# Layer 0's scores of a pair in two PSUM banks, softmax up to four units ahead in the first chunk, and positions set anew

## The chip, the cores and the metric

The kernel runs on one core of one Trainium2 chip. The metric is the device time of one execution in microseconds (us). The program is one launch; its engines are TensorE (PE), VectorE (DVE), ScalarE (ACT), GpSimd (POOL) and SyncE (SP, which only issues DMAs). Each engine works through its own list of instructions in order and meets the others at semaphores.

## The reference

Four layers run one after the other on x (8 sequences of 256 tokens, 512 features). Cut to what matters:

```python
# layer 0: RMS norm with conditioning, 8 query heads of 64 and ONE key/value head, rope, then a gated MLP
q, k, v = h @ Wq.T, h @ Wk.T, h @ Wv.T
scores = rope(q) @ rope(k).T / 8          # 256 x 256 of each head and sequence
attn = softmax(scores, axis=-1)
x = x + (attn @ v) @ Wo.T
x = x + (silu(h2 @ Wg.T) * (h2 @ Wu.T)) @ Wd.T     # 2048 wide
# layer 1: layer norm, 16 heads of 32, normalised q and k, attention and a gelu MLP of 2048
# layer 2: layer norm, 16 query heads and 4 key heads of 32, sparse mask, attention, no MLP
# layer 3: 8 expert blocks, layer norm, silu, projection
```

Inputs and outputs are float32. A softmax needs the maximum of each row of scores, the exponentials, their sum, and a division.

## The kernel before

**Tiling.** The 2048 tokens are four batches of 512 (two sequences each), features lie on the partitions. Attention of layer L on batch n is an *item*; `ORDER` has 12 items, the first four are layer 0 on batches 0 to 3 (called chunks here). An item is 16 *units* g: four groups t of heads, two sequences b, two query tiles of 128 tokens (the last bit of g). Units g and g+1 with g even are a *pair*: same heads, same sequence. A large matmul is taken as three products of rounded halves, so a projection of 128x512 is 12 matmuls.

**Steps of a unit, by the name in the plan.** `scores` (for a pair: 12 matmuls in layer 0, two heads of 64) on PE; `softmax`: on DVE a `reduce_max` per head and a multiply by -0.125 into NM, then on ACT an exponential per head from PSUM to a buffer of SS, with its sum; `normalise`: reciprocal of the sum on DVE, a multiply of each head by it on POOL; `turn`: four transposes of a bank on PE, and a copy to PT by ACT (g even) or DVE (g odd) in layer 0; `values` (for a pair, one unit after its second turn): 8 matmuls, then copies to CX by ACT and DVE; after an item, `out` (48 matmuls). Projections of q and k: `ro1` (12 matmuls, copied out by ACT), `ro2` (rotation matmul, sine product and sum on DVE, cosine product on POOL), `qs` (rounded part on DVE, rest on POOL) or `ks`; in layer 1 `un1`, `un2`, `un3` stand in their place. `split` (POOL) prepares a weight piece that came by `load`, `store` and `fetch` (SP) keep and bring it back.

**Order.** Nothing schedules at run time. `Plan.at` gives every step a position, in units; the steps are sorted by it, and every engine walks the one list and emits its part of each step. `unit(g)` stands at position g and adds, in this order: scores of g+2 (if even), normalise g+1, values g-3 (if g is odd), turn g, softmax g+2 (`AHEAD = 2`). The table `PLACE` holds the positions of everything else. Chunk 0 has no MLP to run beside it; from chunk 1 on the MLP of the batch before stands between the units.

**Memory.** PSUM has 8 banks of 128x512 float32, given out by the pool `dp` first in, first out; the next user of a bank waits for the last reader of the one before. A pair of layer 0 takes four banks of which each holds one head of one unit in its first 256 columns; layers 1 and 2 also take four, with a head's two units side by side. SS has three buffers of probabilities, taken in turn (`ssr`), NM four sets of maxima and sums. HM is the MLP's input (rounded part and rest, 16 KB of a partition); it is first written by the last norm steps (`nfin`) of the MLP of batch 0, at position 19.7.

## Time and profile before

| | us |
|---|---|
| median of 3 runs (2042.67 to 2044.4) | 2044.22 |
| span of the profiled execution | 2053.7 |
| PE busy in it | 1912.4 (93%) |
| DVE / ACT / POOL busy | 1110.8 / 1027.7 / 795.9 |

The profiled execution's span is 9.5 us above the median of the timed runs, so a difference read in the trace is carried over to the median as a difference, not as a ratio. In the profile each engine has its busy time; a wait is idle time of an engine just before an instruction, named by what released it. Times in the trace are counted from the start of the span.

### The profile page before, as it was taken

The numbers are of one execution on the slowest core, as the hardware profiler recorded it, in microseconds if no ns is written. First come the engines' busy times: TensorE is split into PE (matmuls) and PEld (weight loads), VectorE is DVE, ScalarE is ACT, GpSimd is POOL, SyncE is SP. The second block draws the span as 40 slices with busy tenths as digits, with TensorE's granted clock in tenths as the row PEclk, the third lists the DMA queues.
The fourth block names the chain that finished last, engine by engine and source line by source line (L and its number), as shares of the span: only waits on it lengthen the run. The fifth ranks groups of instructions, "written<-read, shape, count | busy, mean of one in ns | idle before, by whom it ended". The sixth has DMA issues, their size and how long they took to land.

```text
span 2053.7 us, 35242 instructions
## 1 busy us (share of the span) xinstructions
PE 1912.4 (93%) x12880; PEld 1512.5 (74%) x12880; DVE 1110.8 (54%) x3184; ACT 1027.7 (50%) x2474; POOL 795.9 (39%) x1094
## 2 busy tenths in 40 slices
PE   5889999999999999999899989989999989988987
PEld 3567777788888878887778777768876768855565
DVE  5655535644553365345664676574554675366363
ACT  3542423433343344443565465555567565468665
POOL 4556662111124243234667554326332432243230
PEclk9899999999999999999999999989999999989989
DMA  7336677555444534444345433433433335322311
GB/s 249 110 129 209 229 249 264 181 196 190 172 160 177 181 134 171 156 158 153 135 174 187 158 118 139 171 114 107 165 113 134 127 110 195 130 81 69 124 63 52
DMA packets 98795, 314.84 MB, mean 153 GB/s; under 512 B 11584, under 2 KB 13376, under 8 KB 97088
## 3 DMA queue, kind: packets, MB, share of 16 engines
q1 hardware_dynamic: 98624, 312.58, 43.7%
q8 instruction: 104, 1.70, 0.3%
q14 instruction: 67, 0.55, 0.1%
HBM read 242.55 MB, written 66.58 MB: 151 GB/s over the span
## 4 chain that ended last, share of the span: by engine, by line
PE 76%; DVE 10%; POOL 4%; ACT 4%; issue 3%; DMA 1%; SPq 0%; POOLq 0%; DVEq 0%; ACTq 0%
PE B L194 69%; PE B L197 7%; DVE FB L215 2%; POOL R L212 1%; DVE SS L218 1%; DVE T L212 1%; POOL SS L209 1%; ACT SS L200 1%; DVE FB L212 1%; POOL FB L212 1%; DMA ST<-in_wpack 1%; DVE PT L206 1%; ACT FB L200 1%; DVE HA L215 1%; POOL W L212 1%
## 5 line engine op out<-in xcount | busy, mean ns | idle before, releaser
L209 POOL TENSOR_SCALAR SS<-SS,NM 128x256 f32<-128x256 f32 (+1 forms) x640 | 290.2, 471 | 747.3 <-DVE NM L224 747.1
L194 PE MATMUL B<-HM,W 128*128 128x512 f32 x2304 | 540.1, 395 | 9.2 <-DVE HM L215 5.7
L194 PEld LDWEIGHTS B<-HM,W 128*128 128x128 f32 x2304 | 436.5, 190 | 105.6 <-issue 5.0
L194 PE MATMUL B<-G,W 128*128 128x512 f32 x1536 | 391.6, 405 | 8.1 <-POOL W L212 4.3
L194 PEld LDWEIGHTS B<-G,W 128*128 128x128 f32 x1536 | 286.1, 191 | 76.1 <-issue 10.7
L200 ACT ACTIVATE SS<-SS,NM 128x256 f32<-128x256 f32 (+1 forms) x512 | 240.5, 471 | 121.2 <-DVE NM L218 120.8
L194 PE MATMUL B<-HA,W 128*128 128x512 f32 x864 | 229.6, 418 | 6.1 <-DVE HA L212 4.4
L197 PE MATMUL B<-ident,SS 128*128 128x128 f32 x1152 | 180.6, 294 | 41.1 <-POOL SS L209 33.6
L194 PEld LDWEIGHTS B<-HA,W 128*128 128x128 f32 x864 | 170.6, 202 | 45.9 <-issue 5.4
L212 DVE TENSOR_TENSOR G<-FB,G 128x512 fp32r<-128x512 f32 x128 | 99.5, 780 | 165.3 <-ACT G L200 165.2
L197 PEld LDWEIGHTS B<-ident,SS 128*128 128x128 f32 x1152 | 129.9, 147 | 77.6 <-issue 41.1
L212 POOL TENSOR_TENSOR R<-R,few 128x16 f32<-128x16 f32 (+2 forms) x57 | 119.3, 2095 | 141.5 <-DVE R L209 141.4
L200 ACT ACTIVATE PT<-B 128x512 f32<-128x512 f32 x160 | 95.0, 593 | 149.6 <-PE B L197 147.4
L212 POOL TENSOR_TENSOR W<-ST,W 128x512 fp32r<-128x512 f32 x119 | 159.8, 1343 | 9.9
L200 ACT ACTIVATE G<-FB 128x512 fp32r<-128x512 f32 x128 | 80.9, 632 | 162.3 <-DVE FB L212 160.3
L209 POOL TENSOR_SCALAR W<-ST 128x512 fp32r<-128x512 f32 x119 | 80.3, 675 | 201.4 <-PE B L194 125.2
L212 DVE TENSOR_TENSOR FB<-FB,B 128x512 f32<-128x512 f32 x64 | 44.0, 687 | 191.5 <-PE B L194 175.8
L200 ACT ACTIVATE FB<-B 128x512 f32<-128x512 f32 (+2 forms) x148 | 85.6, 592 | 105.3 <-PE B L194 104.8
L194 PE MATMUL B<-CX,W 128*128 128x512 f32 (+1 forms) x624 | 136.3, 376 | 0.3 <-issue 0.3
L212 DVE TENSOR_TENSOR X<-X,B 128x512 f32<-128x512 f32 (+1 forms) x100 | 66.4, 665 | 128.8 <-PE B L194 128.7
L200 ACT ACT_TABLE_LOAD x99 | 127.0, 1283 | 4.8 <-PE B L194 2.4
L194 PEld LDWEIGHTS B<-CX,W 128*128 128x128 f32 x624 | 111.3, 190 | 22.8 <-issue 1.9
(109 smaller groups left out, 2654.0 us busy)
## 6 DMA issues: line engine op xcount, KB each, us to landing
W<-kept SPq DMA_DIRECT2D x357, 512.0 KB, 4.2
kept<-W SPq DMA_DIRECT2D x119, 512.0 KB, 4.6
ST<-in_wpack SPq DMA_DIRECT2D x139, 256.0 KB, 2.9
Y<-in_adaw SPq DMA_DIRECT2D x12, 1024.0 KB, 6.8
FB<-FB SPq DMA_DIRECT2D x52, 64.0 KB, 2.6
X<-in_xT SPq DMA_DIRECT2D x1, 3072.0 KB, 13.0
out_xT<-X SPq DMA_DIRECT2D x12, 256.0 KB, 2.1
FB<-in_pos SPq DMA_DIRECT2D x4, 256.0 KB, 6.0
```

Source lines behind the costliest of these rows:

```text
L194: return self.real.matmul(*a, **k) if self.real is not None else self
L197: return self.real.transpose(*a, **k) if self.real is not None else self
L200: return self.real.activation(*a, **k) if self.real is not None else self
L206: return self.real.tensor_copy(*a, **k) if self.real is not None else self
L209: return self.real.tensor_scalar(*a, **k) if self.real is not None else self
L212: return self.real.tensor_tensor(*a, **k) if self.real is not None else self
L215: return self.real.scalar_tensor_tensor(*a, **k) if self.real is not None else self
L218: return self.real.tensor_tensor_reduce(*a, **k) if self.real is not None else self
```

## The change

1. **Two banks for a pair of layer 0.** The scores of a pair now lie as in the other layers: one bank for a head, the first unit in columns 0 to 255, the second in 256 to 511. With the even unit DVE reads both: two `reduce_max` of 2x256 and one multiply for both units; with the odd unit DVE does nothing. Both banks come free with the odd unit's exponentials.
2. **Softmax further ahead in chunk 0.** `ahead(g)` is 4 for units 0 to 9, 3.5, 3 and 2.5 for the pairs 10, 12 and 14, and 2 from unit 16 on (the last pair's value is 2 too, so nothing is deepened at the end). Scores and softmax get positions of their own, `normalise` of a deep unit moves one unit earlier, and the projections of q and k move with `ahead`.
3. **Buffers.** SE overlaps HM's memory and gives two more buffers of probabilities for units below 16. NM has six sets. The first writing of HM waits for the last transposes of unit 15. The waits of the later MLP inputs are named by the right key (before, the key named nothing and no wait was made); the matmul waited for lies 40 to 94 steps ahead of the first one that waits, in both plans.
4. **Positions.** About half of the numbers in `PLACE` change, most of them by less than 0.3 of a unit. Beside chunk 0 this swaps some neighbours; the 16 `un2` of q in layer 1 stand some steps earlier, and in the last item two `second` come before two `out`.

```diff
 AHEAD = 2
+DEEP = 4
+FIRST_DEEP, LAST_DEEP = 16, 192
 LAG = 2
...
 PLACE = {
...
-    "q1": [-1.273, 0.351, 1.427],
+    "q1": [-1.247, -0.466, 1.37],
-    "start": [-12.43, 6, -2.831, -0.049],
+    "start": [-12.43, 7.191, -2.895, 0.384],
...
+def deep(g):
+    return g < FIRST_DEEP or g >= LAST_DEEP
+def ahead(g):
+    return min(DEEP, max(AHEAD, AHEAD + (FIRST_DEEP - pair(g)) / 4, AHEAD + 0.5 + (pair(g) - LAST_DEEP) / 4))
+def banks_of(g):
+    return keys(g) * HEADS[layer(g)] // 512
 def keys(g):
...
-    def __init__(self, dp, f, nm, ss):
-        self.dp, self.f, self.nm, self.ss = dp, f, nm, ss
-        self.work, self.steps, self.raw_values = [], [], {}
+    def __init__(self, dp, f, nm):
+        self.dp, self.f, self.nm = dp, f, nm
+        self.ss_free, self.ss_user, self.banks = list(range(5)), {}, {}
+        self.work, self.steps, self.raw_values, self.ss_of = [], [], {}, {}
...
+    def scores(self, g):
+        self.banks[g] = [self.dp.take() for _ in range(HEADS[layer(g)])]
+        self.add("scores", g, self.banks[g])
+    def softmax(self, g):
+        k = next(k for k in self.ss_free if k < 3 or deep(g))
+        self.ss_free.remove(k)
+        self.ss_of[g] = k, self.ss_user.get(k)
+        self.ss_user[k] = g
+        us = self.banks[pair(g)]
+        self.add("softmax", g, us, self.ss_of[g], self.nm.take())
+        if g % 2:
+            self.dp.give(*us)
     def unit(self, g):
-        a = g + AHEAD
-        if a < UNITS and a % 2 == 0:
-            self.banks = [self.dp.take() for _ in range(4)]
-            self.add("scores", a, self.banks)
-        if 0 <= g + 1 < UNITS:
-            self.add("normalise", g + 1)
+        for a in (g + 1, g + 2):
+            if 0 <= a < UNITS and a - g == (2 if ahead(a) > 3 else 1):
+                self.add("normalise", a)
         if g % 2 and g > 1:
...
         if 0 <= g < UNITS:
-            us = [self.dp.take() for _ in range(keys(g) * HEADS[layer(g)] // 512)]
+            us = [self.dp.take() for _ in range(banks_of(g))]
             self.add("turn", g, us)
             self.dp.give(*us)
-        if a < UNITS:
-            us = self.banks if layer(a) else self.banks[2 * (a % 2):2 * (a % 2) + 2]
-            self.add("softmax", a, us, self.ss.take(), self.nm.take())
-            if layer(a) == 0 or a % 2:
-                self.dp.give(*us)
+            self.ss_free.append(self.ss_of[g][0])
...
-        s = 16 * ITEM[L, n] + 4 * t - 4 - AHEAD
+        s = 16 * ITEM[L, n] + 4 * t - 4 - ahead(16 * ITEM[L, n] + 4 * t)
         s += 1 if L == 1 and t == 0 else PLACE["start"][3] if (L, n, t) == (0, 0, 1) else 0
...
             self.over(ada[i], [x, x + 1])
-        for g in range(-AHEAD, UNITS + LAG):
+        for g in range(0, UNITS, 2):
+            self.at(g - ahead(g) - 0.002, self.scores, g)
+        for g in range(-DEEP, UNITS + LAG):
             self.at(g, self.unit, g)
+        for g in range(UNITS):
+            self.at(g - ahead(g) + 0.001, self.softmax, g)
         for k in range(ITEMS):
...
         HA = sb("HA", [128, 2, 4, 512], F32R)
-        HM = sb("HM", [128, 2, 4, 512], F32R)
+        with nc.sbuf_tensor("HM", [128, 2, 4, 512], F32R) as HM:
+            pass
+        SE = sb("SE", [128, 4, 4, 256])
         G = sb("G", [128, 4, 2, 512], F32R)
...
         SM = sb("SM", [128, 4])
-        NM = sb("NM", [128, 4, 12])
+        NM = sb("NM", [128, 6, 8])
         R4 = sb("R4", [128, 8])
...
         fr = Pool([FB[:, i, :] for i in range(FBUFS)])
-        nmr = Ring([NM[:, i, :] for i in range(4)])
-        ssr = Ring([SS[:, i] for i in range(3)])
+        nmr = Ring([NM[:, i, :] for i in range(6)])
+        ssb = [SS[:, i] for i in range(3)] + [SE[:, i] for i in range(2)]
...
-        plan = Plan(dp, fr, nmr, ssr)
+        plan = Plan(dp, fr, nmr)
         plan.make()
...
                 last_projection[s[1:3]] = ("v", *s[1:5])
-        ss_of = {s[1]: s[3] for s in plan.steps if s[0] == "softmax"}
         nm_of = {s[1]: s[4] for s in plan.steps if s[0] == "softmax"}
...
                 return p_qkv.of(*last_projection[b, n])
-            return p_up.of(4 * L + n - 1, 3, 3)
+            if (L, n) == (0, 0):
+                return p_tr.of(FIRST_DEEP - 1, banks_of(FIRST_DEEP - 1) - 1)
+            q = 4 * L + n - 1
+            return p_up.of(q, 3, 3, 1 if q < 4 else 0)
...
+        after_mlps = [s[3] for s in plan.steps if s[0] == "softmax" and s[1] >= LAST_DEEP
+                      and (s[3][1] is None or s[3][1] < LAST_DEEP)]
+        def probabilities_free(su):
+            k, before = su
+            waits = [p_tr.of(before, banks_of(before) - 1)] if before is not None else []
+            if k > 2 and su in after_mlps:
+                waits.append(p_up.of(7, 3, 3, 0))
+            return waits
         def number(n, *name):
...
                                 p = slice(rows * h, rows * h + rows)
-                                o = dp.buf(us[2 * qt + h])[:, 0:w] if L == 0 else dp.buf(us[h])[:, 256 * qt:256 * qt + w]
+                                o = dp.buf(us[h])[:, 256 * qt:256 * qt + w]
                                 r = e.matmul(o, Q[p, i % 2, x, qs], KB[p, b, y, 0:w], start=(x + y == 0), stop=(x == 1))
...
                     per = 4 // nh
-                    s = ssr.buf(ss_of[g])
+                    s = ssb[plan.ss_of[g][0]]
                     for k, u in enumerate(us):
...
                     L, w, nh = layer(g), keys(g), HEADS[layer(g)]
-                    nm, s = nmr.buf(nu), ssr.buf(su)
-                    e.wait_ge(*nmr.over(nu))
-                    e.wait_ge(*p_sc.of(pair(g)))
-                    if L == 0:
+                    nm, s = nmr.buf(nu), ssb[su[0]]
+                    if L == 0 and g % 2 == 0:
+                        both = NM[:, nu % 6:nu % 6 + 2, :]
+                        e.wait_ge(*nmr.over(nu))
+                        e.wait_ge(*nmr.over(nu + 1))
+                        e.wait_ge(*p_sc.of(g))
                         for j, u in enumerate(us):
-                            r = e.reduce_max(nm[:, j:j + 1], dp.buf(u)[:, 0:256], AX)
+                            r = e.reduce_max(both[:, :, 4 + j], halves(dp.buf(u)[:, :]), AX)
                         r.then_inc(*d_max.up(g, 0))
                         e.wait_ge(*d_max.of(g, 0))
-                        e.tensor_scalar(nm[:, 4:4 + nh], nm[:, 0:nh], -SCORE[L], None, ALU.mult).then_inc(*d_neg.up(g))
-                    else:
-                        e.wait_ge(*ssr.over(su))
+                        e.tensor_scalar(both[:, :, 0:nh], both[:, :, 4:4 + nh], -SCORE[L], None,
+                                        ALU.mult).then_inc(*d_neg.up(g))
+                    elif L:
+                        e.wait_ge(*nmr.over(nu))
+                        e.wait_ge(*p_sc.of(pair(g)))
+                        for wait in probabilities_free(su):
+                            e.wait_ge(*wait)
                         for hh in range(nh):
...
                                 out=s[:, hh, 0:w], in0=dp.buf(u)[:, q:q + w], in1=bias,
-                                scale=-SCORE[L], scalar=3.0e38, op0=ALU.add, op1=ALU.min, accum_out=nm[:, 4 + hh:5 + hh])
+                                scale=-SCORE[L], scalar=3.0e38, op0=ALU.add, op1=ALU.min, accum_out=nm[:, hh:hh + 1])
                             if hh % 2:
...
                         e.wait_ge(*a_exp.of(g, p))
-                        e.reciprocal(nm[:, hs[0]:hs[-1] + 1], nm[:, 8 + hs[0]:9 + hs[-1]]).then_inc(*d_rec.up(g, p))
+                        e.reciprocal(nm[:, hs[0]:hs[-1] + 1], nm[:, 4 + hs[0]:5 + hs[-1]]).then_inc(*d_rec.up(g, p))
                 elif kind == "turn":
...
                     g, us, su, nu = a
-                    L, w, nh = layer(g), keys(g), HEADS[layer(g)]
-                    nm, s = nmr.buf(nu), ssr.buf(su)
-                    e.wait_ge(*ssr.over(su))
+                    L, w, nh, q = layer(g), keys(g), HEADS[layer(g)], 256 * (g % 2)
+                    nm, s = nmr.buf(nu), ssb[su[0]]
+                    for wait in probabilities_free(su):
+                        e.wait_ge(*wait)
                     for p, hs in enumerate(groups(g)):
-                        e.wait_ge(*(d_max.of(g, p) if L else d_neg.of(g)))
+                        e.wait_ge(*(d_max.of(g, p) if L else d_neg.of(pair(g))))
                         for hh in hs:
-                            src, scale = (s[:, hh, 0:w], -1.0) if L else (dp.buf(us[hh])[:, 0:256], SCORE[0])
-                            r = e.activation(s[:, hh, 0:w], src, ACT.Exp, bias=nm[:, 4 + hh:5 + hh], scale=scale,
-                                             accum_out=nm[:, 8 + hh:9 + hh])
-                            if L == 0:
+                            src, scale = (s[:, hh, 0:w], -1.0) if L else (dp.buf(us[hh])[:, q:q + 256], SCORE[0])
+                            r = e.activation(s[:, hh, 0:w], src, ACT.Exp, bias=nm[:, hh:hh + 1], scale=scale,
+                                             accum_out=nm[:, 4 + hh:5 + hh])
+                            if L == 0 and g % 2:
                                 dp.done(us[hh], a_exp, g, 0)
...
                             dp.done(u, a_pt, g, k)
-                    ssr.done(ss_of[g], p_tr, g, len(us) - 1)
                 elif kind == "values":
...
                     w, nh, nm = keys(g), HEADS[layer(g)], nmr.buf(nm_of[g])
-                    s = ssr.buf(ss_of[g])
+                    s = ssb[plan.ss_of[g][0]]
                     for p, hs in enumerate(groups(g)):```

What stands in a row on three engines at the start of chunk 0. Names: `HA,W` is a projection (`ro1`), `KB,Q` scores of a pair, `FB,rotm` a rotation, `ident,SS` or `ident,SE` turns, `PT,V` values; line numbers are shifted by two in the changed kernel.

PE at the start of chunk 0, before, from the projection of q of t = 1 on:

```order
L194 MATMUL B<-HA,W 128x512 x12
L194 MATMUL B<-KB,Q 128x256 x12
L194 MATMUL B<-FB,rotm 128x512
L194 MATMUL B<-KB,Q 128x256 x12
L197 MATMUL B<-ident,SS 128x128 x8
L194 MATMUL B<-HA,W 128x512 x12
L194 MATMUL B<-KB,Q 128x256 x12
L197 MATMUL B<-ident,SS 128x128 x4
L194 MATMUL B<-FB,rotm 128x512
L194 MATMUL B<-PT,V 64x128 x8
```

and in the changed kernel:

```order
L196 MATMUL B<-HA,W 128x512 x12
L196 MATMUL B<-KB,Q 128x256 x12
L196 MATMUL B<-FB,rotm 128x512
L199 MATMUL B<-ident,FB 128x64 x4
L196 MATMUL B<-KB,Q 128x256 x12
L196 MATMUL B<-HA,W 128x512 x12
L196 MATMUL B<-KB,Q 128x256 x12
L199 MATMUL B<-ident,SS 128x128 x4
L196 MATMUL B<-FB,rotm 128x512
L199 MATMUL B<-ident,SS 128x128 x4
L196 MATMUL B<-KB,Q 128x256 x12
```

The first turns stood behind the second scores; now a projection and the third scores stand between them.

DVE in the same place, before, from the first reciprocal (unit 0) on (TENSOR_REDUCE is the maximum, COPY PT the odd unit's copy):

```order
L224 RECIPROCAL NM<-NM 128x2
L221 TENSOR_REDUCE NM<-B 128x1 x2
L209 TENSOR_SCALAR NM<-NM 128x2
L224 RECIPROCAL NM<-NM 128x2
L221 TENSOR_REDUCE NM<-B 128x1 x2
L209 TENSOR_SCALAR NM<-NM 128x2
L224 RECIPROCAL NM<-NM 128x2
L206 COPY PT<-B 128x512
L221 TENSOR_REDUCE NM<-B 128x1 x2
```

and in the changed kernel, from the maxima of the second pair on:

```order
L223 TENSOR_REDUCE NM<-B 128x2 x2
L211 TENSOR_SCALAR NM<-NM 128x2x2
L226 RECIPROCAL NM<-NM 128x2 x2
L223 TENSOR_REDUCE NM<-B 128x2 x2
L211 TENSOR_SCALAR NM<-NM 128x2x2
L214 TENSOR_TENSOR FB<-B,TR 128x512
L214 TENSOR_TENSOR FB<-FB 128x512
L208 CAST Q<-FB 128x512
L226 RECIPROCAL NM<-NM 128x2
L208 COPY PT<-B 128x512
```

Between the last two of these COPY and REDUCE rows lies the difference: a maximum no longer stands behind the copy of an odd unit, but that copy (the first one) now stands behind the rotation of q of t = 2.

POOL in the same place, from the weight pieces before the first q on; SS and SE rows are `normalise`, W rows `split`, FB rows the cosine product and Q rows the rest of q. Before:

```order
L212 TENSOR_TENSOR Q<-FB,Q 128x512
L209 TENSOR_SCALAR SS<-SS,NM 128x256 x6
L209 TENSOR_SCALAR W<-ST 128x512
L212 TENSOR_TENSOR W<-ST,W 128x512
L209 TENSOR_SCALAR SS<-SS,NM 128x256 x2
L212 TENSOR_TENSOR FB<-FB,TR 128x512
L212 TENSOR_TENSOR Q<-FB,Q 128x512
L209 TENSOR_SCALAR SS<-SS,NM 128x256 x6
```

and in the changed kernel:

```order
L214 TENSOR_TENSOR Q<-FB,Q 128x512
L211 TENSOR_SCALAR SS<-SS,NM 128x256 x4
L211 TENSOR_SCALAR W<-ST 128x512
L214 TENSOR_TENSOR W<-ST,W 128x512
L211 TENSOR_SCALAR SS<-SS,NM 128x256 x2
L214 TENSOR_TENSOR FB<-FB,TR 128x512
L214 TENSOR_TENSOR Q<-FB,Q 128x512
L211 TENSOR_SCALAR SE<-SE,NM 128x256 x4
```

The kinds of work stand in the same order; unit 2 (not 3) is the one between `split` and the rotation of q, and unit 3 stands behind that rotation.

## Rows read from the trace of the kernel before

**Rows 1.** The page: busy time of each engine, share of the span, instructions.

```profile
PE 1912.4 (93%) x12880; PEld 1512.5 (74%) x12880; DVE 1110.8 (54%) x3184; ACT 1027.7 (50%) x2474; POOL 795.9 (39%) x1094
```

**Rows 2.** Windows: stretch and length; busy us by engine; PEclk, DMA share, GB/s.

```profile
37.00:121.00 84.00, 65.10 (x451) 47.93 (x451) 54.30 (x145) 42.20 (x118) 46.30 (x63) 0.82 0.39 130
141.00:350.00 209.00, 200.30 (x1198) 159.98 (x1197) 101.52 (x223) 72.43 (x152) 111.85 (x123) 0.96 0.66 225
350.00:950.00 600.00, 594.12 (x3685) 489.44 (x3686) 289.92 (x739) 245.09 (x553) 164.29 (x214) 1.00 0.49 173
```

**Rows 3.** PE's waits from 40 to 141 us: total, times, longest.

```profile
PE B L197 <- POOL SS L209: 13.3, 9, 3.8
PE B L194 <- DVE PT L206: 3.9, 2, 2.4
PE B L197 <- POOL R L212: 2.1, 1, 2.1
PE B L197 <- ACT SS L200: 1.7, 2, 0.8
```

**Rows 4.** PE's timeline: start, us, instruction group, [idle before, releaser].

```profile
37.56 1.65 PE L194 MATMUL B<-KB,Q 64*128 64x256 f32 x12 [3.44 <-issue]
...
46.16 1.11 PE L197 MATMUL B<-ident,SS 128*128 128x128 f32 x4 [3.78 <-POOL SS L209]
...
66.33 5.47 PE L194 MATMUL B<-HA,W 128*128 128x512 f32 x12
...
97.62 1.09 PE L194 MATMUL B<-PT,V 128*64 128x128 f32 x16
98.64 0.66 PE L197 MATMUL B<-ident,SS 128*128 128x128 f32 x4
99.14 1.02 PE L194 MATMUL B<-FB,rotm 128*128 128x512 f32 x2
...
109.73 0.97 PE L194 MATMUL B<-KB,Q 64*128 64x256 f32 x12
...
112.99 0.66 PE L197 MATMUL B<-ident,SS 128*128 128x128 f32 x4 [0.68 <-POOL SS L209]
113.58 0.97 PE L194 MATMUL B<-KB,Q 64*128 64x256 f32 x12
...
117.73 0.63 PE L197 MATMUL B<-ident,SS 128*128 128x128 f32 x4 [1.56 <-POOL SS L209]
118.11 3.00 PE L194 MATMUL B<-HA,W 128*128 128x512 f32 x12
121.10 11.17 PE L194 MATMUL B<-CX,W 128*128 128x512 f32 x48
...
136.40 0.63 PE L197 MATMUL B<-ident,SS 128*128 128x128 f32 x4 [1.62 <-POOL SS L209]
```

**Rows 5.** All engines' timeline: what lies between turn 15 and turn 17.

```profile
113.76 0.68 DVE L206 COPY PT<-B 128x512 f32<-128x512 f32 x1
114.36 0.75 DVE L221 TENSOR_REDUCE NM<-B 128x1 f32<-128x256 f32 x2
...
115.34 0.47 ACT L200 ACTIVATE SS<-B,NM 128x256 f32<-128x256 f32 x1 [1.96 <-DVE NM L209]
...
116.40 0.17 DVE L224 RECIPROCAL NM<-NM 128x2 f32<-128x2 f32 x1 [1.09 <-ACT SS L200]
...
116.65 0.93 POOL L209 TENSOR_SCALAR SS<-SS,NM 128x256 f32<-128x256 f32 x2 [2.32 <-DVE NM L224]
```

**Rows 6.** DVE's groups by form, 37 to 121 us: count, busy, mean ns, idle before.

```profile
L221 DVE TENSOR_REDUCE NM<-B 128x1 f32<-128x256 f32 x38 | 14.2, 416 | 11.6 <-PE B L194 11.6
L209 DVE TENSOR_SCALAR NM<-NM 128x2 f32<-128x2 f32 x19 | 5.4, 285 | 0.6
L212 DVE TENSOR_TENSOR FB<-FB 128x512 f32<-128x512 f32 x6 | 4.2, 692 | 5.8 <-POOL FB L212 5.8
L212 DVE TENSOR_TENSOR CX<-B,CX 128x256 fp32r<-128x256 f32 x8 | 3.3, 414 | 1.3 <-ACT CX L200 1.0
```

**Rows 7.** Timelines of DVE and POOL at 74 us; compare POOL's 0.93 in rows 5.

```profile
73.86 2.45 DVE L215 SCALAR_TENSOR_TENSOR FB<-FB 128x512 f32<-128x512 f32 x3
...
73.90 1.87 POOL L209 TENSOR_SCALAR SS<-SS,NM 128x256 f32<-128x256 f32 x2
```

**Rows 8.** SP's queue: the loads around the conditioning weights (`load ada`).

```profile
56.17 1.06 SPq L227 DMA_DIRECT2D Y<-in_adaw  x1
73.95 0.33 SPq L227 DMA_DIRECT2D ST<-in_wpack  x1
```

**Rows 9.** PE's waits over the whole span on ACT's wide factors (`un3`).

```profile
PE B L197 <- ACT FB L200: 4.7, 3, 1.8
```

52 lines of the change are left out of this document (26 added, 26 removed), and 20 rows, old and new, of the table PLACE.

## The prediction

> **What bounds the kernel now.** Read the page's busy times first [rows 1]: PE is busy 93% of the span, DVE, ACT and POOL about half and less, so only time in which PE stands idle, or works at the lower clock, can be won. The windows say where that is [rows 2]. From 350 to 950 us (layer 0 with its MLPs, then the first of layer 1) PE is busy 594.12 of 600 us: 5.9 us are left. From 37 to 121 us, chunk 0, it is busy 65.1 of 84 us at a granted clock of 0.82 of full. That is the stretch the change aims at. PE's waits of the chunk and the steps behind it [rows 3] name POOL's SS most: a turn waits for `normalise`, 13.3 us in nine waits. So a chain is short of time, not an engine: in the same window DVE is busy 54.3 and POOL 46.3 of 84 us.
>
> The chain can be followed for one unit [rows 4, 5]. Turn 15 runs on PE at 112.99. Its copy to PT starts on DVE at 113.76, and only behind it does DVE take the maxima of unit 17 (114.36), although their scores (109.73) had been on PSUM since about 110.7; exponentials 115.34, reciprocal 116.40, POOL 116.65, turn 17 at 117.73. So turn g leads to turn g+2 in 4.74 us for an odd unit, whatever PE has. With the lead of 2 this loop binds wherever PE has less than that to do between the two.
>
> How much is to be had: from the first scores at 37.56 to the first `out` at 121.10 are 83.5 us [rows 4]. PE's own work in it at full clock, by distances of starts in the same rows: 6 projections of 3.0 (118.11 to 121.10), 10 scores of 0.9, 8 values of 1.02, 18 turns of 0.5, 5 rotations of about 1.0, and about 3.6 for norms, ada and small transposes: 18 + 9 + 8.2 + 9 + 4.9 + 3.6 = 52.7 us. The other 30.8 us are idle time, 18.4 (84 - 65.1 of the window [rows 2], less half a us ahead of 37.56), and slow clock, about 12.4: the projection at 66.33 took 5.47 us, the same 12 matmuls took 3.00 at 118.11 [rows 4]. The clock falls behind idle gaps, so both go together: about 0.7 us of slow clock for a us of gap.
>
> **The change, part by part.**
>
> Softmax ahead in chunk 0. Between the scores of a pair and its first turn stand now, counted in the same durations, 2 to 9.5 us of PE work; in the changed kernel 7 to 15 us. The chain from maxima to the end of POOL's product is 3.2 us (114.36 to 117.6 [rows 5]), so it is covered with room for queueing. What stays: (a) at the start nothing can be ahead: the scores of unit 0 wait for q as before, and PE is slow for some us: 3.0. (b) In the order of DVE, unit 1's copy stands behind the rotation of q of t = 2, which waits for POOL's cosine product, and on POOL unit 3's product stands behind that rotation's rest: 0.5 and 2.0. (c) On SP `load ada` 1 was issued at 56.17, ahead of the load that follows `split` 12 (73.95) [rows 8]; it now stands behind the store of that split, which I place at about 60, while PE wants the weights at about 68: 1.5, at most the time of a transfer. (d) The projections of batch 1 wait for the last norm steps, which DVE does in one go: 1.5. (e) DVE, POOL and PE still meet in order; I allow 0.3 for each of 18 turns, below the 0.68 of turn 15 [rows 4]: 5.4. Sum 52.7 + 3.0 + 2.5 + 1.5 + 1.5 + 5.4 = 66.6, against 83.5: **16.9 us won**. Ends: 27.5 if only (a) stays, 8 if half of the gaps and their clock stay.
>
> DVE has to fit too: it did 54.3 us in the window; 5.8 of waiting for the cosine product stay [rows 6]. With what the next part saves it has about 49 + 5.8 + 3 = 58 us in 66.6. It fits, but is nearly full, which is why I keep (e).
>
> Two banks for a pair. Before, a pair cost DVE 4 maxima of 0.416 and 2 products of 0.285, 2.23 us; now 2 maxima of twice the length and 1 product. The trace has no maximum of 2x256; for twice the length a TENSOR_TENSOR goes from 0.414 to 0.692 [rows 6], a factor of 1.67, so 0.70 each and 1.68 for the pair (between 1.12 with no growth and 1.95 with full growth): 0.55 saved, 5 us in chunk 0, none of it on the path by itself. What counts is the loop: an odd unit's maxima are made with the even one's, so neither turn 17's wait of 1.56 nor that of turn 19 (1.62 at 136.40) [rows 4] has the maxima behind a copy any more. The first is in the sum above; the second is **1.6 more**. Against it the even unit's exponentials start 2 x (0.70 - 0.416) = 0.57 us later. In the 24 pairs with lead 2 in layer 0 other work covers this: PE has 5.9 idle us in 600 [rows 2]. Taken as 0, at most 13.7. The banks: a pair holds two instead of four, a little longer; the waits for ACT's SS (1.7 [rows 3]) are of that kind and can only shrink.
>
> Buffers. The first MLP input waits for turn 15; it stands 48 steps behind it and its PE work comes after all of `out` (11.17 us [rows 4]): 0. The waits with the right key lie 40 steps and more behind their cause: 0. Weight pieces for `out` and the first MLP are split when a slot comes free, which PE's own projections decide, so they move along with PE: 0; from 141 to 350 us POOL is busy 112 of 209 us and DMA 0.66 [rows 2].
>
> Positions. In layer 1 `un2` closes up to `un1` (from 6 to 33 us of PE work down to 1.6 to 24) and stands further ahead of `un3`, whose waits are 4.7 us in all [rows 9]; 0, between 3 won and 5 lost. The rest swaps neighbours: 0.
>
> Sum: 16.9 + 1.6 = 18.5 us less. The profiled span is 2053.7, it would be 2035.2; the median goes from 2044.2 to **2025.7**, say 2026.
>
> **A collision the rows show.** The product of `normalise` takes POOL 0.93 for a unit [rows 5], but 1.87 at 73.90 while DVE ran three operations on FB [rows 7]. The changed order packs DVE and POOL denser, so more of these may meet. The Trainium skill has a rule for it (SBUF — State Buffer, "Who interferes with whom"): GpSimd and VectorE share one pair of ports as an exclusive lock, and a VectorE operation with two SBUF inputs or in a two-port mode makes the other wait for its whole length. By that rule it is not bandwidth but each meeting that costs, and this trace agrees at 73.90; it is rival 2 below.
>
> **Rivals.**
>
> 1. The ideal: the clock stays up and (b) to (e) shrink to under 2 us in all. For it: 5 buffers and up to 15 us of cover. Against: DVE's 58 us. Gain 27.5 + 1.6 less that 2: about 2017, range 2010 to 2018.
> 2. DVE and POOL become the bound of the chunk. If 12 of 18 products take 0.94 longer [rows 5, 7], POOL has 11.3 us more on a path that is then tight: gain 7 to 8, 2037 (2034 to 2040). For it: DVE nearly full, in-order waits on both. Against: ten products in the window took 0.93 for two heads next to DVE work.
> 3. The gain is given back: PE reaches the MLP of batch 0 earlier and waits there for its weights. For: DMA 0.66 in that stretch. Against: POOL's half-idle time. 2041 to 2047.
> 4. Slower: the even units of the 24 pairs with lead 2 miss their turn by the 0.57 us, 13.7 us of gaps, and gaps take clock with them at 0.7 for 1, so 23 us against 18.5: 2049. It decides from four fifths of these pairs on. For: these turns follow each other closely in the plan. Against: 5.9 idle us in 600 us today, with the MLP's matmuls in between.
>
> **How the numbers follow.** Forecast 0.52 (2026, own range 2018 to 2034), rival 1 0.12, rival 2 0.18, rival 3 0.08, rival 4 0.10. The range takes the forecast, rival 2 and most of rival 1: 2012 to 2040. About 0.2%, 4 us, is what a measurement of this kernel can tell from no change. Faster by more: 0.52 + 0.12 + 0.18 = 0.82; within: 0.08; slower: 0.10.
>
> **What would show it.** In the profile of the changed kernel the first `out` starts at 102 to 107 us, not 121; the granted clock from 48 to 100 us is above 0.9; PE's waits for POOL's SS in chunk 0 sum to under 5 us; a maximum takes 0.65 to 0.75 and no turn of layer 0 shows the 4.74 us loop. From `out` on the same steps should come 17 to 20 us earlier to the end of the span. Wrong would be: POOL products of 1.8 us in most units (rival 2); the gap at `out` shrinking in the next 200 us (3); new waits of turns of even units from 141 to 900 us (4).

## The result and the profile after

The changed kernel takes 2042.14 us (median of 19 runs, 2032.31 to 2045.91) against 2047.24 for the kernel before (19 runs, 2039.58 to 2053.31). The ratio of the two kernels is 0.9967, with a 95% interval from 0.9955 to 0.9978: 6.8 us less, between 4.5 and 9.2 (the two medians by themselves lie 5.1 us apart). The sign was right and the mechanism in chunk 0 is there, but the size was not: 18.5 us were forecast.

The busy times of DVE, ACT and POOL are those of before within 4 us; PE's is 12.4 us lower for the same 12880 matmuls. DVE has 96 instructions less, the maxima and products that two banks save [rows 1]. From the page:

```profile
PE 1900.0 (93%) x12880; PEld 1505.2 (74%) x12880; DVE 1107.2 (54%) x3088; ACT 1026.0 (50%) x2474; POOL 792.9 (39%) x1094
```

The windows of the changed kernel: chunk 0 (first scores to first `out`), the stretch from there to the first `up` of the second MLP, the rest of layer 0 up to the `out` of layer 1's first item, and the stretch behind it; columns as in [rows 2].

```profile
37.80:113.20 75.40, 60.80 (x455) 45.22 (x455) 51.63 (x118) 43.29 (x124) 44.50 (x62) 0.87 0.41 144
113.20:344.10 230.90, 218.58 (x1342) 175.23 (x1343) 115.29 (x224) 79.76 (x174) 125.48 (x143) 0.98 0.67 228
344.10:931.40 587.30, 582.71 (x3614) 480.57 (x3612) 280.77 (x685) 241.29 (x545) 163.38 (x212) 1.00 0.49 170
931.40:1184.20 252.80, 239.32 (x1762) 198.01 (x1762) 158.18 (x452) 131.59 (x326) 158.88 (x195) 0.97 0.49 171
```

The first `out` starts at 113.25, not at 102 to 107. PE is idle 14.6 us in chunk 0, and the granted clock is 0.87. Its waits from 40 to 133 us, where [rows 3] had 13.3 us in nine waits for SS:

```profile
PE B L196 <- DMA Y<-in_adaw: 4.4, 1, 4.4
PE B L199 <- POOL SS L211: 3.9, 4, 2.0
PE B L199 <- POOL SE L211: 2.9, 2, 2.3
PE B L196 <- ACT FB L202: 1.7, 2, 1.5
PE B L196 <- DVE PT L208: 1.7, 1, 1.7
...
PE B L199 <- DVE BI L208: 1.3, 1, 1.3
```

So the waits for `normalise` fell from 13.3 to 6.8 us, and the turn loop of [rows 5] is gone. Up to the first `out` alone, before had

```profile
PE B L197 <- POOL SS L209: 11.6, 8, 3.8
```

and the changed kernel

```profile
PE B L199 <- POOL SE L211: 2.9, 2, 2.3
PE B L199 <- POOL SS L211: 1.9, 3, 1.0
```

which is 4.8 us; the other 2.0 us are turn 19, behind `out`. In their place stand the conditioning weights (Y), for whose load PE waits 4.4 us, and behind them the BI copy. PE's timeline there, and the turn 19 that was to be freed:

```profile
73.44 1.52 PE L196 MATMUL B<-Y,CT 128*32 128x128 f32 x32 [4.42 <-DMA Y<-in_adaw]
74.89 1.11 PE L199 MATMUL B<-ident,SE 128*128 128x128 f32 x4
77.27 0.48 PE L199 MATMUL B<-ident,BI 128*128 128x128 f32 x1 [1.26 <-DVE BI L208]
77.67 1.65 PE L196 MATMUL B<-KB,Q 64*128 64x256 f32 x12
79.25 1.80 PE L196 MATMUL B<-PT,V 128*64 128x128 f32 x16
...
113.25 11.12 PE L196 MATMUL B<-CX,W 128*128 128x512 f32 x48 [0.76 <-issue]
...
128.88 0.63 PE L199 MATMUL B<-ident,SS 128*128 128x128 f32 x4 [1.99 <-POOL SS L211]
```

Scores and values behind the gap took 1.65 and 1.80 us, where [rows 4] has 0.97 and 1.09 for the same work: the slow clock again. The wait at turn 19 is 1.99 us, not gone (before: 1.62 [rows 4]). What it waits for is on POOL: the product of unit 19 stands behind a `split` and takes 1.92 us for its two heads, where others take 0.94, beside three squares (T) on DVE. The changed kernel's POOL and DVE:

```profile
126.82 1.92 POOL L211 TENSOR_SCALAR SS<-SS,NM 128x256 f32<-128x256 f32 x2
```

```profile
126.82 2.45 DVE L214 TENSOR_TENSOR T<-T 128x512 f32<-128x512 f32 x3
```

and those of before, ahead of its turn 19 at 136.40:

```profile
134.39 1.87 POOL L209 TENSOR_SCALAR SS<-SS,NM 128x256 f32<-128x256 f32 x2
```

```profile
134.35 2.44 DVE L212 TENSOR_TENSOR T<-T 128x512 f32<-128x512 f32 x3
```

DVE from 68 to 78 us, without a pause of more than 0.1 us: the last steps of the angles of batch 1 (FB), with a reciprocal of `normalise` and a pair's maxima between them, then norm steps (FB<-X,ADA,B) and the BI copy.

```profile
68.40 0.42 DVE L208 CAST FB<-FB 128x512 f32<-128x512 int32 x1
68.85 1.37 DVE L211 TENSOR_SCALAR FB<-FB,CV 128x512 f32<-128x512 f32 x1
70.25 0.89 DVE L211 TENSOR_SCALAR FB<-FB 128x512 f32<-128x512 f32 x2
71.06 0.16 DVE L226 RECIPROCAL NM<-NM 128x2 f32<-128x2 f32 x1
71.14 1.27 DVE L223 TENSOR_REDUCE NM<-B 128x2 f32<-128x512 f32 x2
72.44 0.17 DVE L211 TENSOR_SCALAR NM<-NM 128x4 f32<-128x4 f32 x1
72.52 2.13 DVE L217 SCALAR_TENSOR_TENSOR FB<-FB 128x512 f32<-128x512 f32 x3
...
76.15 0.86 DVE L217 SCALAR_TENSOR_TENSOR FB<-X,ADA,B 128x256 f32<-128x256 f32 x2
76.93 0.28 DVE L208 COPY BI<-B 128x128 f32<-128x128 f32 x1
```

The windows of 6 us show DVE as nearly full there: it is busy 10.9 of 12 us, PE 6.3.

```profile
67.00:73.00 6.00, 2.02 (x24) 1.61 (x24) 5.50 (x11) 0.36 (x1) 2.54 (x4) 1.00 0.63 248
73.00:79.00 6.00, 4.30 (x49) 3.30 (x49) 5.41 (x15) 5.94 (x16) 1.88 (x4) 0.58 0.00 0
```

Both traces against each other, step by step: the first `out` comes 7.85 us earlier, the second 10.2, the fifth (943 us before) 11.4, and the end 15.3. The two profiled executions flatter the change, though: before's span of 2053.7 lies 8 us above its median run, the changed kernel's 2038.4 lies 2 below. What belongs to the program takes more traces to find.

### The profile page after: what moved, and what is told of

The parts are those of the page before. It is cut to its first block, busy times and chain, and to the rows that moved or that the text cites. A ratio compares the mean times of both kernels' runs of the same rounds, so it can differ in the third digit from the quotient of the medians.

```text
span 2038.4 us, 35133 instructions
## 1 busy us (share of the span) xinstructions
PE 1900.0 (93%) x12880; PEld 1505.2 (74%) x12880; DVE 1107.2 (54%) x3088; ACT 1026.0 (50%) x2474; POOL 792.9 (39%) x1094
## 4 chain that ended last, share of the span: by engine, by line
PE 77%; DVE 10%; POOL 5%; ACT 3%; issue 3%; DMA 2%; SPq 0%; POOLq 0%; DVEq 0%; ACTq 0%
PE B L196 70%; PE B L199 7%; DVE FB L217 2%; DVE T L214 1%; POOL R L214 1%; POOL SS L211 1%; DVE SS L220 1%; ACT SS L202 1%; POOL W L214 1%; DMA ST<-in_wpack 1%; DVE FB L214 1%; DVE HA L217 1%; DVE X L217 1%; POOL FB L214 1%; ACT GF L202 1%
## 5 line engine op out<-in xcount | busy, mean ns | idle before, releaser
L211 POOL TENSOR_SCALAR SS<-SS,NM 128x256 f32<-128x256 f32 (+1 forms) x628 | 286.1, 474 | 711.2 <-DVE NM L226 711.0
L196 PE MATMUL B<-HM,W 128*128 128x512 f32 x2304 | 538.3, 394 | 12.6 <-DVE FB L217 3.9
L196 PEld LDWEIGHTS B<-HM,W 128*128 128x128 f32 x2304 | 434.9, 190 | 109.3 <-issue 10.5
L196 PE MATMUL B<-G,W 128*128 128x512 f32 x1536 | 390.6, 404 | 8.4 <-POOL W L214 4.2
L196 PEld LDWEIGHTS B<-G,W 128*128 128x128 f32 x1536 | 285.0, 191 | 75.4 <-issue 9.5
L202 ACT ACTIVATE SS<-SS,NM 128x256 f32<-128x256 f32 (+1 forms) x512 | 240.5, 471 | 118.5 <-DVE NM L220 118.0
L196 PE MATMUL B<-HA,W 128*128 128x512 f32 x864 | 221.9, 407 | 7.3 <-DVE HA L214 5.5
L196 PEld LDWEIGHTS B<-HA,W 128*128 128x128 f32 x864 | 165.2, 195 | 45.0 <-DVE HA L214 3.9
L199 PE MATMUL B<-ident,SS 128*128 128x128 f32 x1128 | 170.9, 288 | 27.7 <-POOL SS L211 23.3
L214 DVE TENSOR_TENSOR G<-FB,G 128x512 fp32r<-128x512 f32 x128 | 103.3, 810 | 155.0 <-ACT G L202 155.0
L214 POOL TENSOR_TENSOR R<-R,few 128x16 f32<-128x16 f32 (+2 forms) x57 | 118.9, 2088 | 166.4 <-DVE R L211 166.4
L199 PEld LDWEIGHTS B<-ident,SS 128*128 128x128 f32 x1128 | 123.7, 144 | 62.4 <-issue 34.3
L202 ACT ACTIVATE G<-FB 128x512 fp32r<-128x512 f32 x128 | 80.9, 632 | 174.5 <-DVE FB L214 172.5
L214 POOL TENSOR_TENSOR W<-ST,W 128x512 fp32r<-128x512 f32 x119 | 159.3, 1339 | 9.9
L202 ACT ACTIVATE FB<-B 128x512 f32<-128x512 f32 (+2 forms) x148 | 86.0, 593 | 140.0 <-PE B L196 139.6
L202 ACT ACTIVATE PT<-B 128x512 f32<-128x512 f32 x160 | 95.0, 594 | 121.0 <-PE B L199 119.1
L211 POOL TENSOR_SCALAR W<-ST 128x512 fp32r<-128x512 f32 x119 | 78.8, 662 | 178.8 <-PE B L196 112.8
L214 DVE TENSOR_TENSOR FB<-FB,B 128x512 f32<-128x512 f32 x64 | 44.0, 688 | 188.5 <-PE B L196 180.8
L214 DVE TENSOR_TENSOR X<-X,B 128x512 f32<-128x512 f32 (+1 forms) x100 | 66.4, 665 | 136.6 <-PE B L196 136.6
L196 PE MATMUL B<-CX,W 128*128 128x512 f32 (+1 forms) x624 | 137.1, 377 | 1.0 <-issue 1.0
L196 PEld LDWEIGHTS B<-CX,W 128*128 128x128 f32 x624 | 111.5, 190 | 23.5 <-issue 2.8
```

The source lines that it names most:

```text
L196: return self.real.matmul(*a, **k) if self.real is not None else self
L199: return self.real.transpose(*a, **k) if self.real is not None else self
L202: return self.real.activation(*a, **k) if self.real is not None else self
L211: return self.real.tensor_scalar(*a, **k) if self.real is not None else self
L214: return self.real.tensor_tensor(*a, **k) if self.real is not None else self
```

## The experiments

Each median stands beside that of before in the same group of runs; medians of different groups are compared only through their ratios to before. "Chunk 0" is from the first scores to the first `out`; "stretch 2" from there to the first `up` of the second MLP (some expectations wrongly call this point the third `up`); "stretch 3" to the `out` of layer 1's first item; "stretch 4" to the first `up` of the MLP behind, near 1190 us. A row of stretches without a count of traces is one trace.

### Second and third traces of both kernels

Both kernels unaltered.

> The changed kernel once more, unaltered, so that the others of this group have it on the same chip, and so that its trace tells how far a stage moves between two executions of one program. In the first trace the first `out` started at 113.25 us (before: 121.10), the first `up` at 135.1 (143.6), and the end came 15.3 us earlier, while the medians are only 5 to 7 us apart. Theory A (what the change is worth is chunk 0's 8 us, no more; the other 7 us of the trace are a difference of the clock between the two profiled executions): median 5 to 8 us under before, first `out` again at 113 +- 0.5, and the differences behind chunk 0 wander by several us against the first trace. Rival B (the later 7 us are real and are lost in the other executions): the same later steps come 15 to 20 us earlier than before again, and the median is 12 or more under.

> The kernel before once more, unaltered, for its trace. The one I predicted from had a span of 2053.7 us, some 8 above the timed median less the 1.9 around a span. Theory A (such a difference is the granted clock behind the gaps of layers 1 and 2): first `out` again at 121 +- 0.7, the steps up to 940 us within 2 us of the first trace, and what differs lies behind 940 us. Rival B (the first trace was slow in chunk 0 already, so that part of the changed kernel's 7.85 us there was never real): first `out` at 118 or earlier.

> The kernel before, a third trace. Chunk 0 (first scores to first `out`) took 83.5 us in the trace I predicted from and 79.1 in the second, with the same idle time (18.3 and 19.1) and a different granted clock (0.82 and 0.87). Theory A (the idle time belongs to the program, the slow clock behind it to the execution): idle 18 to 19.5, length anywhere in 77 to 85. Rival B (83.5 was an outlier): length 78.5 to 80.

> The changed kernel, a third trace. Chunk 0 took 75.4 and 76.7 us, with 14.6 and 14.7 us idle and a clock of 0.87 in both; runs with nearly the same order had 74.5 (idle 17.0, clock 0.90), 75.5 (13.4, 0.85) and 77.5 (14.4, 0.83). Theory A (as for before: idle time is the program's, the clock the execution's): idle 14 to 15.5, length in 73 to 79. Rival B (the length is the program's too): 75 to 77.

Timed again, the changed kernel has 2040.04 us against 2047.57 (0.9965, 0.9952 to 0.9978). Of `same_after`, theory A holds in the time, and its first `out` came at 114.7, 1.2 us outside what A gave; rival B does not hold. Windows of chunk 0: before in the second and the third trace, then the changed kernel in its second and third:

```profile
36.60:115.70 79.10, 60.00 (x451) 44.67 (x452) 55.05 (x145) 42.26 (x118) 45.90 (x62) 0.87 0.40 138
```

```profile
38.00:118.10 80.10, 61.73 (x452) 45.47 (x452) 54.44 (x145) 42.25 (x118) 45.84 (x62) 0.85 0.40 135
```

```profile
38.00:114.70 76.70, 61.97 (x455) 45.80 (x456) 52.79 (x118) 43.33 (x124) 44.51 (x62) 0.87 0.40 141
```

```profile
38.00:113.60 75.60, 60.32 (x455) 44.81 (x456) 51.52 (x118) 43.41 (x124) 44.36 (x62) 0.87 0.41 143
```

| chunk 0, three traces each | length | PE idle | PE busy |
|---|---|---|---|
| before | 83.5, 79.1, 80.1 | 18.3, 19.1, 18.4 | 65.2, 60.0, 61.7 |
| changed | 75.4, 76.7, 75.6 | 14.6, 14.7, 15.3 | 60.8, 62.0, 60.3 |

The idle time of before is the program's (it varies by 0.8 us); how long the same matmuls take is the execution's (5.2 us). For the changed kernel the three lengths lie so close (75.4 to 76.7) that theory A and rival B of `same_after2` both hold. The projection that took 5.47 us in the trace I predicted from [rows 4] took 3.01 in both others, although the wait of 3 us for SS ahead of it and the short one for T are still there. PE's timeline in the second trace:

```profile
62.94 1.05 PE L194 MATMUL B<-few,T 128*128 128x1 f32 x8 [0.19 <-DVE T L212]
63.86 3.01 PE L194 MATMUL B<-HA,W 128*128 128x512 f32 x12
```

and from the third:

```profile
60.94 0.63 PE L197 MATMUL B<-ident,SS 128*128 128x128 f32 x4 [3.04 <-POOL SS L209]
...
64.93 1.09 PE L194 MATMUL B<-few,T 128*128 128x1 f32 x8 [0.50 <-DVE T L212]
65.88 3.01 PE L194 MATMUL B<-HA,W 128*128 128x512 f32 x12
```

Theory A of `same_before` was right in kind, but not in place: it expected the spread behind 940 us, and of the 7.2 us between the first two traces of before 5.4 lay ahead of the first `out` (121.1 and 115.7), 4.4 of them in chunk 0, where rival B had put it. By the means of three traces each, chunk 0's gain is 80.9 - 75.9 = 5.0 us, and 3.7 of them are idle time (18.6 - 14.9). The Trainium skill (TensorE: Matmul & The Clock Gate, "What's actually happening") says that the number of slow matmuls of one kernel differs from run to run; these traces agree, with 60.0 to 65.2 us for one list of matmuls. It puts the penalty of the ramp at the start under 1% of a typical kernel's span. The 5.2 us here are 0.25% of the span, and yet as much as chunk 0 won.

### Which part of the change brings the time

`lead2` is the changed kernel with

```diff
-DEEP = 4
+DEEP = 2
```

`oldplaces` is the changed kernel with the table `PLACE` of before, `twobanks` has both edits, and `newplaces` is the kernel before with the table of the changed one.

> The changed kernel with DEEP = 2: scores of a pair in two banks, new positions and new buffers stay, but softmax runs two units ahead everywhere, as before. Theory A (the deep lead brings chunk 0's 8 us): first `out` at 119 to 122, median within 2 us of before. Rival B (the two banks and the shorter loop of DVE bring a good part, since an odd unit's maxima no longer stand behind a copy): first `out` at 115 to 117, and the median 3 to 5 under before. Rival C (elsewhere the even units pay for the maxima of 2x256, a loss that chunk 0's gain hides): median 3 to 8 us ABOVE before.

> The changed kernel with the positions (the table PLACE) of before: four units ahead and two banks stay. Theory A (positions are worth nothing outside chunk 0, and inside it they only put back what the lead moved): median within 2 us of the changed kernel. Rival B (the new positions are needed by the deep lead): first `out` at 116 or later, median 3 or more us above the changed kernel. Rival C (the new positions lose time elsewhere, which is where the missing half of my 18 us went): median 3 or more us BELOW the changed kernel, with the same first `out`.

> The changed kernel with DEEP = 2 and the positions of before: what is left of the change is the two banks of a pair (and the buffers, unused). Of the group before: the same with the new positions had its first `out` at 117.4 and a median of 2041.75, the four-unit lead with old positions 114.4 and 2050.7. Theory A (the two banks alone bring the 3 to 4 us of chunk 0 that were seen without the lead, since an odd unit's maxima no longer stand behind a copy): first `out` at 117 to 118.5, median 2 to 4 us under before. Rival B (positions bring them): first `out` at 120 or later, median within 1.5 us of before or above it.

> The kernel before with the changed kernel's table of positions and nothing else. Theory A (the positions carry most of what the whole change is worth in time, 5 to 7 us, since with them a lead of 2 is as fast as a lead of 4, and without them the lead of 4 is no faster than before): median 4 to 7 us under before; the steps behind the first MLP come earlier than in before by more than those of chunk 0 do. Rival B (they only fit together with the new order of chunk 0): median within 2 us of before. I had taken the positions as 0, with ends 3 won and 5 lost.

| | banks, lead, positions | median, before | ratio (95%) | chunk 0 (idle) | stretch 2 | stretch 3 |
|---|---|---|---|---|---|---|
| before | 4, 2, old | | 1 | 80.9 (18.6) | 234.4 | 587.0 |
| newplaces | 4, 2, new | 2048.89, 2047.63 | 1.0016 (0.9999 to 1.0032) | 85.6 (18.8) | 232.3 | 586.1 |
| twobanks | 2, 2, old | 2050.37, 2047.63 | 1.0018 (1.0000 to 1.0036) | 80.4 (16.0) | 234.3 | 589.0 |
| lead2 | 2, 2, new | 2041.75, 2047.57 | 0.9969 (0.9956 to 0.9982) | 79.2 (17.3) | 230.6 | 587.1 |
| oldplaces | 2, 4, old | 2050.70, 2047.57 | 1.0007 (0.9993 to 1.0020) | 77.4 (16.4) | 234.2 | 589.1 |
| changed | 2, 4, new | 2040.04, 2047.57 | 0.9965 (0.9952 to 0.9978) | 75.9 (14.9) | 231.3 | 587.7 |

(before and changed: means of three traces.) The deep lead is worth little in time by itself: 0.9969 with a lead of 2 and 0.9965 with 4, though chunk 0 is 3 us shorter with it, 2.4 of them idle time. The positions alone and the banks alone bring nothing or lose some 3 us (both intervals touch 1); together they bring 6. The two kernels with a lead of 2 and two banks also use the new buffers SE (their turns wait for them in chunk 0), although the expectation of `twobanks` calls them unused. `lead2` came nearest to its rival B (first `out` 117.4, median 5.8 under). `oldplaces` is 10.7 us above the changed kernel of its group, as rival B has it in time, but with the first `out` at 114.4, so most of the loss is not in chunk 0. `twobanks` had its first `out` at 117.2, as theory A, and a median above before, as rival B. `newplaces` is rival B. The rows of stretch 2 and 3, `twobanks` first, then `lead2` (stretch 2):

```profile
117.20:351.50 234.30, 220.17 (x1342) 175.55 (x1343) 114.84 (x224) 80.98 (x175) 126.77 (x143) 0.97 0.66 226
351.50:940.50 589.00, 581.96 (x3606) 479.61 (x3605) 281.03 (x683) 239.74 (x541) 162.43 (x212) 1.00 0.49 169
```

```profile
117.40:348.00 230.60, 218.91 (x1341) 175.40 (x1342) 113.92 (x224) 79.77 (x174) 125.86 (x143) 0.98 0.67 228
```

In stretch 3, two banks with the old positions cost 2 us in every trace that had them (589.0, 589.1, 589.2). PE's waits of `twobanks` there name two that before does not have at this length (BI 0.5, HM 0):

```profile
PE B L199 <- DVE BI L208: 1.7, 1, 1.7
PE B L199 <- ACT FB L202: 1.6, 1, 1.6
PE B L196 <- DVE HM L214: 1.2, 2, 1.0
```

So two banks with the old positions cost 2 us here, and it falls on small steps of DVE (the BI copy, the norm), not on turns. That it is the double maxima of the even unit that push them back is argued, not shown: no run has two banks with the maxima unit by unit. With two banks and the new positions the wait for BI is 0.8 to 1.7, that for HM 0.6, and the stretch is 587 to 588.

### Does the wait for the conditioning weights cost anything?

```diff
-            self.at(x - 2 if i == 1 else x - 2.9, self.add, "load ada", i)
+            self.at(x - 4.4 if i == 1 else x - 2.9, self.add, "load ada", i)
```

> The changed kernel with one position altered: `load ada` 1 stands 2.4 units earlier, so that on SP it comes ahead of the store and the load that wait for `split` 12. In the changed kernel it was issued at 65.48 (before: 56.17), and PE waited 4.4 us for its data at 73.44, with the slow clock behind it for some 3 us more. Theory A (that wait is real time on the path): PE's wait for the DMA of Y is 0 to 0.5, first `out` at 107 to 110, median 3 to 6 us under the changed kernel. Rival B (the time that PE stood there was taken from waits that come anyway: DVE and POOL, late from unit 6 on, set the pace of the next turns): the wait is gone, but waits for SS or SE behind it grow by as much, first `out` at 112 to 113.5, median within 1.5 us.

2040.17 against 2047.57, 0.9967 (0.9951 to 0.9983): nothing won over the changed kernel's 2040.04 in the same group. Rival B holds. The wait for the load is gone, and PE waits instead, in the same place, for a product whose reciprocal stands in DVE's queue and for a copy in that queue:

```profile
66.47 1.08 PE L196 MATMUL B<-Y,CT 128*32 128x128 f32 x32
71.27 1.09 PE L199 MATMUL B<-ident,SE 128*128 128x128 f32 x4 [3.71 <-POOL SE L211]
76.14 0.48 PE L199 MATMUL B<-ident,BI 128*128 128x128 f32 x1 [3.78 <-DVE BI L208]
```

Idle time in chunk 0 even rose to 17.0 us, and yet this is the shortest chunk 0 of all, 74.5 us: the granted clock was 0.90 and PE's busy part 57.5 us:

```profile
37.70:112.20 74.50, 57.53 (x456) 42.62 (x456) 51.81 (x118) 43.03 (x124) 44.39 (x62) 0.90 0.41 146
```

> The kernel before with the new positions and `load ada` 1 early, so without the 3.9 us for which PE waited there for its data when the positions alone were changed (chunk 0, first scores to first `out`, 85.6 us; two traces of before: 83.5 and 79.1). Over all traces so far the stretch from the first `out` to the third `up` of the second MLP took 234.2 to 234.5 us with the old positions (four kernels) and 229.8 to 232.3 with the new ones (six). Theory A (the new positions are worth 5 us behind chunk 0 whatever the banks and the lead are; chunk 0 gave it back): chunk 0 at 79 to 83, the stretch behind at 230 to 232.5, median 3 to 6 us under before. Rival B (the new positions need the two banks): median within 2 us of before.

The same edit in `newplaces`: the wait for the load went, chunk 0 stayed at 84.1 us (idle 20.0, clock 0.82), stretch 2 took 234.0, and the median is 2050.05 against 2048.01, 1.0009 (0.9996 to 1.0021). Rival B: the positions bring nothing without the two banks, and the load was not what held them back.

### Can DVE's jam be taken apart?

Three edits on the changed kernel. `trig_soon` has `load ada` 1 early and the angles of batch 1 earlier:

```diff
-                self.over(self.trig(k + 1), [x, x + 1.55, x + 2.75, x + 4.75])
+                self.over(self.trig(k + 1), [1.9, 3.05, 4.05, 8.89] if k == 0 else [x, x + 1.55, x + 2.75, x + 4.75])
```

`ada_later` has the first number of `PLACE["ada"]` at 12.3 instead of 7.843 and its load at `x - 2.9`; `ada_later_angle` has besides

```diff
-                self.over(self.trig(k + 1), [x, x + 1.55, x + 2.75, x + 4.75])
+                self.over(self.trig(k + 1), [x, x + (1.55 if k else 2), x + (2.75 if k else 3.1), x + 4.75])
```

> The changed kernel with `load ada` 1 early, and besides DVE's part of batch 1's rope angles (`pos`, `angle`, `turns`: 5.2 us of DVE, eight operations) at positions 1.9, 3.05 and 4.05 instead of 4.14, 5.69 and 6.89. In the changed kernel DVE is busy 10.9 of the 12 us from 67 to 79 us and PE 6.3; between 55 and 67 us DVE has 5.6 idle. Theory A (DVE is the bound from 67 to 85 us, and this block of norm and angle work of batch 1 is what the deeper lead runs into): PE's idle time from 60 to 90 us falls by 4 us or more, first `out` at 106 to 109, median 3 to 5 under the changed kernel. Rival B (the loop through POOL and ACT sets the pace, wherever the angles stand): first `out` within 1 us of 112.2, the waits moved to 50 to 65 us.

> The changed kernel with the second group of conditioning values (`ada` 1, `adt` 1, its load; needed only by the MLP norm behind chunk 0) at position 12.3 instead of 7.843, out of the stretch of 67 to 85 us where DVE is busy 10.9 of 12 us with the norm and the angles of batch 1. With the load early only, PE waited there 3.7 us for `normalise` 8 and 3.8 us for a copy of `ada` 1 (BI), and nothing was won. Theory A (what holds PE there is DVE's queue in order, and the copy of BI need not stand in it): chunk 0 at 70 to 73 us (changed kernel: 75.4 and 76.7), median 2 to 5 under the changed kernel's 2040.0 and 2042.1. Rival B (the time goes to the next waits, for SE and SS, since DVE's work is not less): chunk 0 at 74 to 77, median within 1.5 us of it.

> The same as the run with `ada` 1 at 12.3, and besides `angle` and `turns` of batch 1 a third of a unit later (6.14 and 7.24 instead of 5.69 and 6.89), so that the reciprocal of `normalise` 8 stands ahead of DVE's 2.7 us of `angle` and that of `normalise` 9 ahead of `turns`. Theory A (turn 8 waits 3.7 us for just that): that wait under 1.5 us and chunk 0 another 1 to 3 us shorter than without this, at 68 to 72. Rival B (DVE has no time to spare there, so the maxima of the next pair come later by as much): the same chunk 0 within 1 us.

| | median, before | ratio (95%) | chunk 0 | idle | busy | clock |
|---|---|---|---|---|---|---|
| trig_soon | 2044.65, 2047.63 | 0.9984 (0.9970 to 0.9997) | 80.9 | 17.0 | 63.9 | 0.85 |
| ada_later | 2041.00, 2048.01 | 0.9968 (0.9954 to 0.9983) | 75.5 | 13.4 | 62.1 | 0.85 |
| ada_later_angle | 2039.76, 2048.01 | 0.9958 (0.9941 to 0.9975) | 77.5 | 14.4 | 63.1 | 0.83 |

`trig_soon` is slower than the changed kernel by its ratio, though the two intervals overlap a little: the angles now stand ahead of the squares that PE needs (wait for T 2.6 us), and DVE's block from 61 to 67 us (5.65 of 6 us busy) is as full as the one from 67 to 79 was. The two others take away the waits for Y and BI; turn 8 waits 3.4 us in `ada_later` and 2.4 in `ada_later_angle`, instead of 3.7. But the next waits come (HA 2.7, CX 1.8 in `ada_later_angle`), and two projections behind them took 7.60 us, against 5.73 in the changed kernel's first trace. From `ada_later_angle`:

```profile
70.87 0.63 PE L199 MATMUL B<-ident,SE 128*128 128x128 f32 x4 [2.36 <-POOL SE L211]
...
74.24 1.98 PE L196 MATMUL B<-PT,V 128*64 128x128 f32 x16 [1.84 <-DVE CX L214]
...
79.93 7.60 PE L196 MATMUL B<-HA,W 128*128 128x512 f32 x24 [2.67 <-DVE HA L214]
```

Only `ada_later` came out as its rival B. `ada_later_angle` had chunk 0 2 us longer than that, which neither of its theories gave, and `trig_soon` had its first `out` at 117.7, also outside both. What they share is that no theory A held: DVE has about 52 us of work in chunk 0, 10.9 of them in the 12 us from 67 to 79, and each time that one wait was taken away others stood in the next places. Whether DVE's load or the order alone does this, these runs don't separate. That the last one is faster than the changed kernel can't be told from these intervals.

### Which positions

`final1` is `oldplaces` with one number, `a final` of batch 2 at 24.202 instead of 24.462; the `up` that it stands among are the second group of the first MLP. `norms_new` has of the new table only `up`, `up end` and the entries of norms and angles; `rest_new` has all the others. `hybrid` is the changed kernel with the norm entries of layer 1 as before, and with them the four entries of norm steps that hold for both layers (`a stats`, `m stats`, `a parts`, `m parts`); `hybrid_ada` adds the two edits of `ada_later_angle`.

> Four units ahead, two banks, and the old positions but for one number: `a final` of batch 2 at 24.202 instead of 24.462, which puts the last norm steps of that batch among the four first `up` of the second MLP and not behind them. In the traces with the old positions PE waits 2.5 to 3.3 us for HA between 190 and 240 us, with the new ones 0.8. Theory A (this one number carries most of the 3.5 us of the stretch from the first `out` to the third `up` of the second MLP): the wait for HA at most 1 us, the stretch at 231 to 232.5 us instead of 234.2. Rival B (the wait moves elsewhere in the stretch): 233.5 or more.

> Four units ahead and two banks; of the positions those of the norms, the rope angles and the MLP's up (`up`, `up end`, and all that begin with `a`, `m` or `trig`) are new, the others old. With all positions old the kernel is no faster than before, with all new 6 to 8 us. Theory A (the gain is in how DVE's norm steps stand among the MLP's steps: waits for HA, T and HM go): from the first `out` to the third `up` of the second MLP 230 to 231.5 us (old 234.2 to 234.5), median 3 to 6 us under before. Rival B (it is in the other half): 233.5 or more, median within 2 us of before.

> The complement of the run before: projections, `ada`, `out`, the start and layers 2 and 3 at the new positions, norms, angles and `up` at the old ones. Theory A (norms carry the gain): stretch behind the first `out` 233.5 or more, median within 2 us of before. Rival B (projections and `ada` carry it): 230 to 231.5, and 3 to 6 us under before. If both halves bring less than 2 us, the positions work only together.

> The changed kernel with the norm positions of layer 0 new and those of layer 1 (and `up` behind it) as before; all other positions new. With the norms new and the rest old, the stretch behind the first `out` went from 234.4 to 231.3 us but the stretch from 943 to 1200 us rose to 259.9; with the rest new and the norms old the first was 233.5 and the second 249.2 (before: 257.1, 255.8, 255.7; changed kernel: 252.8, 254.1, 255.3). Theory A (the two gains lie in different layers and add up): 230 to 232.5 in the first stretch, 248 to 251 in the second, and a median 3 to 5 us under the changed kernel. Rival B (249.2 was that execution's clock or comes from an interplay with the layer 0 positions): 252 or more in the second, median within 2 us of the changed kernel.

> The same with `ada` 1 at 12.3 and the angles of batch 1 a third of a unit later, which by itself took PE's waits for the load and for BI out of chunk 0 (idle 13.4 and 14.4 us instead of 14.6 to 15.3) but left its length at 75.5 and 77.5 us, with a lower clock (0.85 and 0.83 instead of 0.87), and was 0.9958 of before. Theory A (less idle time pays on average over executions though one trace need not show it): median 1 to 2 us under the run without it. Rival B (the clock takes back what the gaps give): within 1 us, either way.

| | median, before | ratio (95%) | stretch 2 | stretch 4 |
|---|---|---|---|---|
| before (3 traces) | | 1 | 234.4 | 257.1, 255.8, 255.7 |
| changed (3 traces) | 2042.14, 2047.24 | 0.9967 | 230.9, 230.5, 232.4 | 252.8, 254.1, 255.3 |
| final1 | one run | | 234.5 | 257.2 |
| norms_new | 2053.26, 2047.27 | 1.0032 (1.0019 to 1.0044) | 231.3 | 259.9 |
| rest_new | 2045.83, 2047.27 | 0.9994 (0.9980 to 1.0007) | 233.5 | 249.2 |
| hybrid | 2043.32, 2050.05 | 0.9968 (0.9956 to 0.9981) | 232.3 | 247.9 |
| hybrid_ada | 2040.77, 2050.05 | 0.9962 (0.9949 to 0.9976) | 233.3 | 247.9 |

`final1` made the wait for HA go from 3.3 to 1.2 us and put 1.1 for a kept weight in its place; the stretch stayed at 234.5, rival B. In `norms_new` stretch 2 is 3 us shorter, in `rest_new` stretch 4 is 7 us shorter, but neither half is clearly faster than before as a whole (`rest_new` 1.4 us, its interval holds 1), and `norms_new` is 6 us slower. These are differences of single traces, and the spread of one plan is wide: among the eight traces of two-bank kernels with the new table behind chunk 0, stretch 4 took 251.0 (`ada_early`) to 256.3 us (`ada_later`). The 249.2 and the two 247.9 lie below all eight, with 11.4 to 11.7 us idle against 13.1 to 14.6. In stretch 2 the case is weaker: with the norms of layer 0 new, `hybrid_ada` took 233.3 and `newplaces_ada` 234.0. Of the two halves, `rest_new` came out as its theory A; `norms_new` has the stretch of its theory A and a median on the other side. `hybrid` has stretch 2 (232.3) as its theory A had it, and stretch 4 at 247.9, next to the 248 to 251 of the theory, as has `hybrid_ada`:

```profile
931.60:1179.50 247.90, 236.33 (x1763) 195.57 (x1762) 156.40 (x452) 131.27 (x326) 160.20 (x195) 0.99 0.50 174
```

and still the median is that of the changed kernel: what is behind 1180 us took 858 us in it (2037.4 - 1179.5) and 854 in the changed one (2038.4 - 1184.2; 850 and 853 in its other traces). Of these 4 us, 3.2 lie in the last stretch, behind the `out` of the tenth item (278.8 against 275.6 us, and 278.8 again in `hybrid_ada`); the changed kernel's third trace has 277.6 there. What makes them was not followed further. `hybrid_ada` against `hybrid` (0.9962 and 0.9968) can't be told apart.

## Why the prediction came out wrong

**The step that failed: chunk 0's sum has the waits that stay, but not the slow clock behind them.** Terms (a) to (e) are 13.9 us on top of 52.7 us of work at full clock, 66.6 in all. On the mean of three traces the changed kernel's chunk 0 has 14.9 us idle and 61.0 us busy, 75.9 in all. So the waits came out 1.0 us over the sum, and the slow clock, 61.0 - 52.7 = 8.3 us, had no term of its own: only (a) speaks of a slow PE, although the same prediction says that the clock falls behind gaps, at 0.7 us for 1. The miss in chunk 0 is 16.9 - 5.0 = 11.9 us: 8.3 of clock, 1.0 of waits and 2.6 of baseline.

That the waits add up nearly right is in part luck, for the terms don't. The turns' waits for POOL before `out` were 4.8 to 5.2 us in the three traces, where (e) and the 2.0 of (b) had 7.4; PE did not wait for HA, where (d) had 1.5. Against it the load of (c) cost 4.0 to 5.0 instead of 1.5, the wait for a PT copy 1.6 to 1.7 instead of 0.5, and waits for FB from ACT (1.4 to 1.7) and for BI (0.4 to 2.2) had no term. Of the ends given for the sum, "27.5 if only (a) stays" should be 83.5 - 55.7 = 27.8, and half of the 30.8 us staying would leave 15 won, not 8.

**The baseline was one execution.** "The other 30.8 us are idle time, 18.4, and slow clock, about 12.4" holds for the trace that I had. In the two others the slow part is 60.0 - 52.7 = 7.3 and 61.7 - 52.7 = 9.0. On the mean chunk 0 begins at 80.9 us, not 83.5: 2.6 of the 16.9 us were never there. The median of before was also of three runs: 2044.2, where 19 runs have 2047.24.

**"About 0.7 us of slow clock for a us of gap" is no rate.** Among the traces with a lead of 4, 17.0 us idle went with 57.5 us busy, 14.6 with 60.8 and 13.4 with 62.1. These are 4.8, 8.1 and 9.4 us above the 52.7, so 0.28 to 0.70 for a us of gap; on the means it is 0.52 for before and 0.56 for the changed kernel. The same rule made rival 4 dear, by 9.6 of its 23 us.

**The check on DVE.** "It fits, but is nearly full" was said of the whole chunk. The norm and the angles of batch 1 are one block; from 67 to 79 us DVE is busy 10.9 of 12 us and PE 6.3, and 5.7 of the 14.6 idle us (Y and BI) lie there. Five kernels moved single steps of it and its load, and chunk 0 stayed between 74.5 and 80.9. An engine's fit has to be checked in the windows in which the work falls, not over the chunk.

**Term (c), 1.5 us for `load ada` 1.** The mechanism was right (it stands behind the store of `split` 12), the size not: issued at 65.5 instead of about 60, it cost 4.4 us. `split` 12 itself was late, behind a product of POOL that waited for a reciprocal. But in `ada_early`, without this wait, nothing is won, so it is not by itself the cause of the miss.

**Turn 19, 1.6 us.** Its wait is 1.99 us, and the reading of it was wrong. Before, the reciprocal of unit 19 was done at 133.1 and PE's turn came at 136.40; between them POOL finished a `split` at 134.4 and took 1.87 us for the product, beside DVE's squares. No maximum lies on that path. The changed kernel has the same picture: reciprocal done at 125.2, `split` until 126.8, product 1.92, turn at 128.88. Two banks could not have removed it.

**Two banks.** The maximum of 2x256 takes 0.68 us by DVE's groups by form of the changed kernel, from 37 to 121 us (estimate 0.70; before 0.416 for half of it [rows 6]):

```profile
L223 DVE TENSOR_REDUCE NM<-B 128x2 f32<-128x512 f32 x20 | 12.8, 683 | 6.4 <-PE B L196 6.4
```

"Taken as 0, at most 13.7" for the even units: the runs show 2 us, on BI and HM and only with the old positions, and not surely from the maxima.

**Positions, 0 (3 won to 5 lost).** This term failed too, the other way. With two banks they are worth 9 to 10 us (0.9965 against 1.0007, 0.9969 against 1.0018), without them nothing, or a loss of up to 3. So the lead and the banks, to which the prediction gave all of the 18.5 us, bring nothing with the old positions (1.0007, 0.9993 to 1.0020); but the old numbers had been set for the old order, so that run doesn't price them alone. The text on the change also makes the table's part too small: 147 of its 211 numbers differ, 27 of them by 0.3 of a unit or more. Going through them by neighbours that swap did not give the sum over layer 0's norms (3 to 4 us in stretch 2), stretch 3 (1 to 2 us), layer 1 (0 to 3 us in stretch 4) and the end.

**Rivals.** POOL's products took 0.48 us a head for SS and 0.50 for SE in the changed kernel from 37 to 121 us and 0.50 before, so rival 2's collisions are not there in most units, though its gain (7 to 8 us) was the nearest: that is luck. For the rule of the Trainium skill cited there (SBUF — State Buffer, "Who interferes with whom") this means: meetings happen, one of them at turn 19 in both kernels, but denser packing did not make them more frequent. Nothing was given back at the MLP's weights (rival 3): stretch 2 is shorter, not longer. Of rival 4 the runs show at most 2 of its 13.7 us, and in stretch 3 no turn that waits.

What was right: the turn loop is broken, waits for `normalise` in chunk 0 fall from 11.6 to 4.8 us ("under 5" was said), a maximum takes 0.68 us (0.65 to 0.75), and the effect is a gain. The other signs did not come: the clock from 48 to 100 us is 0.87 (before 0.77), not above 0.9, and behind `out` the steps come 8 to 15 us earlier in the first traces, not 17 to 20. What stays open is why the positions pay only together with the banks, which of them do, and how much of the clock's loss a given order of gaps brings on the mean; one trace a kernel can't tell either.

## What to carry to other kernels

Take a second and a third trace of the kernel before, ahead of pricing a stretch with many gaps: here the idle time repeated within 0.8 us of 19, while the time that the same matmuls took differed by 5.2 us of 60. Price a gap that closes at its own length, and the clock behind it between nothing and the full difference, and give the gaps that stay their share of slow clock as well. And when a change mixes a structural part with positions tuned for it, neither can be costed alone: here each half by itself was no gain, and only together did they bring the 7 us.

## What was not expected of the hardware

One list of matmuls, with 18.3 to 19.1 us of waits in it, ran at a granted clock of 0.82, 0.87 and 0.85 over 80 us, and one projection of 12 matmuls took 5.47, 3.01 and 3.01 us. Over the whole kernel the executions of one program roughly follow their mean granted clock: of the changed kernel's 19, the three shortest spans (2030.5 to 2033.0 us) had 0.972 to 0.974, and those of 2042 us and more 0.964 to 0.967. A kernel with less idle time in a stretch (13.4 against 17.0 us) was not shorter there (75.5 against 74.5), since the busy part grew by 4.6 us.
